# Context attention in bf16 stacks, self-attention splits read from PSUM, and two streams merged by a table of run lengths

## The chip, the cores and the metric

The kernel runs on one core of one Trainium2 chip. The metric is the device time of one launch in microseconds (us). The kernel before took 3042.41 us, the median of three runs between 3033.93 and 3052.46 us.

## What is computed

The reference is a decoder of four layers over x (4 batches, 512 tokens, width 128) with a context of 77 tokens per batch. Each layer has a self attention, a cross attention and a feed-forward part, twelve stages in all, and after each stage the sum with x is normalised. The stages that the change touches are these (cut):

```python
# self attentions of layers 0 and 1: 16 heads of width 8, causal; layer 3 adds biases and a rotation of q and k
scores = softmax(q @ k.T * HD ** -0.5 (causal));  out = scores @ v
# cross attentions of layers 1 and 2: 16 heads of width 8, 512 queries against the 77 context tokens
qh = x @ wq + bq;  kh = ctx @ wk + bk;  vh = ctx @ wv + bv
out = softmax(qh @ kh.T * scale) @ vh;  x = layernorm(x + out @ wo + bo)
```

## The kernel before

**Streams.** Batches 0 and 2 form stream 0, batches 1 and 3 form stream 1; each stream runs its two batches one after the other through the twelve stages of `STAGES` (L2444) and `add_norm` (L373) after each. Each stream owns four PSUM banks and its own buffers, so the streams share only the engines. Every stage is a `Program`: for each engine a generator that issues instructions between `yield`s of due times, numbers that its author planned by hand.

**Order.** `weave` (L293) merges the two streams on each engine: it issues the part whose due time is lowest, with stream 1's times put back by `LAG` = 60 (L26, L2554 to L2570). Each engine then runs its instructions in that one order, and a wait at its head holds up both streams.

**Self attention** (`attention8`, L463; stages l0_attn, l1_attn, l3_attn). q and k are projected as f32 (L524), copied from PSUM by ScalarE (L620, or L622 with a bias), and split into three bf16 parts each: keys by GpSimd, queries by VectorE (`split_up`, L657 to L668); ScalarE repeats parts (L637). SyncE lays six parts and two pad slots out as stacks of 128 rows for each pair of heads (24 transfers, L606 and L608), so that one bf16 matmul gives an exact score. Scores (L552) have their maxima taken by VectorE (L718 causal, L721 otherwise); the negated maxima are split, turned (L557) and written as rows into the query stacks (L613). A second pass computes the scores transposed (L569), ScalarE takes the exponentials (L648), GpSimd masks (L691), TensorE multiplies with the values (L579).

**Context attention** (`attention8_context`, L1308; stages l1_xattn and l2_xattn, so eight times in a launch). ScalarE makes four copies of q with the other heads zeroed (L1419), VectorE the masked keys (L1449). A score unit is one f32 matmul of 308 columns (L1374, 16 of them), whose maxima VectorE takes (L1461). The maxima are split once (L1464 to L1469), turned (L1379) and copied (L1424). In the second pass each head has one f32 matmul of 512 columns (L1387) and one bf16 matmul that adds its maximum (L1390); ScalarE takes the exponential (L1431) and TensorE multiplies with the values (L1398). SyncE and GpSimd have no part in it.

**Elsewhere.** `add_norm` has GpSimd compute the inverse deviation (L401, L403) and TensorE turn x (L409). l2_ffn (L2098) has GpSimd sum scores (L2205), VectorE and ScalarE mark them (L2278, L2238) and TensorE add them up (L2179).

Of the kernel before, what the change touches and what calls it, by code (L numbers as in the profile page):

```python
# [10 lines left out]
BF16 = mybir.dt.bfloat16  # L11
# [5 lines left out]
P = 128  # L17
B, T, D = 4, 512, 128
TJ = T // P
LC = 77  # L20
# [5 lines left out]
LAG = 60.0  # L26
# [5 lines left out]
PAIR_GROUPS = ((0, 1), (1, 2), (2, 4), (4, 8))  # L32
HEADS8, HD8 = 16, 8


def host_constants():
# [14 lines left out]
    c["quadcol"] = np.kron(np.eye(4, dtype=np.float32), np.ones((32, 1), np.float32))  # L51
    c["quadhalf"] = 0.5 * c["quadcol"]
    selhead = np.zeros((P, 4, 4, LC), np.float32)
    for q in range(4):
        for g in range(4):
            selhead[32 * q + 3 * g:32 * q + 3 * g + 3, q, g, :] = 1
    c["selhead"] = selhead.astype(mybir.dt.np(BF16))
# [235 lines left out]
def weave(tracks):  # L293

    heads = []
    for i, steps in enumerate(tracks):
        t = next(steps, None)
        if t is not None:
            heads.append((t, i, steps))
    while heads:  # L300
        head = min(heads, key=lambda h: h[0:2])
        heads.remove(head)
        t, i, steps = head
        after = next(steps, None)
        if after is not None:
            assert after >= t - 1e-6, (t, after)
            heads.append((after, i, steps))
# [155 lines left out]
def attention8(s, wq, wk, wv, scale, causal=False, bq=None, bk=None, bv=None, rope=False, wo=None, first_wait=None):  # L463

    H, G, KC = HEADS8, HEADS8 // 4, TJ
    T1 = 16.0 if rope else 10.0
# [6 lines left out]
        qk_projected=2, v_projected=1 if wv is not None else 0, qk_biased=2, rotated=2 if rope else 0, rope_chain=4 if rope else 0,  # L473
# [125 lines left out]
    def sync(sp):  # L599
        yield T1 - 2  # L600
# [14 lines left out]
    def scalar(a):  # L615
        for q, bias in ((1, bk), (0, bq)):
            yield 2 - q
            a.wait_ge(*qk_projected(2 - q))
            if bias is None:
                a.copy(qk[:, q, :], bank[q][:]).then_inc(qk_biased.sem, 1)  # L620
            else:
                a.activation(qk[:, q, :], bank[q][:], ACT.Identity, bias=bias).then_inc(qk_biased.sem, 1)  # L622
        yield 3
# [8 lines left out]
        for n in range(2):  # L632
            for q, name, split, repeated in ((1, "k", keys_split, keys_repeated), (0, "q", queries_split, queries_repeated)):
                yield T1 - 5 + 2 * n + 0.5 * (1 - q)
# [21 lines left out]

    def split_up(eng, q, done):  # L657
# [12 lines left out]
    def gpsimd(g_):  # L670
# [5 lines left out]
        yield T1 - 6  # L676
        g_.wait_ge(*(roped if rope else qk_biased)(1))
        for _ in split_up(g_, 1, keys_split):
            yield T1 - 4
# [14 lines left out]
    def vector(v):  # L694
# [8 lines left out]
        yield T1 - 4  # L703
        v.wait_ge(*(roped if rope else qk_biased)(2))
        for _ in split_up(v, 0, queries_split):
            yield T1 - 3
# [601 lines left out]
def attention8_context(s, wq, wk, wv, scale, bq, bk, bv, wo, bo, query_mask=None):  # L1308

    H, G, nk = HEADS8, HEADS8 // 4, LC  # L1310
    x_ready, xT_ready, mask_ready = s.x_ready, s.xT_ready, s.mask_ready
    units = [(j, q) for j in range(TJ) for q in (0, 2, 1, 3)]
    D1, D2 = 0.6, 1.7
    T1 = 6.0
    plan = []
    for n in range(len(units)):
        plan += [(T1 + D1 * n, "score", n), (T1 + D1 * n + 1.0, "max", n)]
    Tm = T1 + D1 * len(units) + 1.0
    plan += [(Tm, "split", 0), (Tm + 1.5, "turn", 0), (Tm + 2.2, "rows", 0)]
    T2 = Tm + 3.0  # L1320
    for m in range(H // 2):
        b = T2 + D2 * m
        plan += [(b, "st", m), (b + 0.8, "exp", m)]
        if m % 2 == 1:
            plan += [(b + 2.2, "pv", m // 2), (b + 3.0, "gather", m // 2), (b + 3.6, "out", m // 2), (b + 4.2, "att", m // 2)]
    plan.sort(key=lambda step: step[0])
    end = plan[-1][0]
    (projected, q_ready, keys_ready, v_ready, scores_ready, scores_read, chain, max_split, max_turned, max_copied, st_ready, exp_done, pv_done,
# [18 lines left out]
    def score_bank(u):  # L1347
        return bank[u % 4][:, 0:4 * nk]
# [4 lines left out]
    def group(n):  # L1353

        return n // 2 % 2 + 2 * (n % 2)
# [1369 lines left out]
```

## Time and profile before

| quantity | value |
|---|---|
| median of three runs | 3042.41 us |
| the profiled execution, its own time | 3028.01 us |
| span of its instructions | 3026.3 us |
| TensorE busy | 2467.5 us |
| VectorE busy | 1779.2 us |
| ScalarE busy | 1301.2 us |
| GpSimd busy | 688.8 us |
| granted TensorE clock, mean share of full speed | 0.891 |

The span runs from the first to the last instruction of the profiled execution, its own time has 1.7 us more around it, and the median of the runs lies 14.4 us above that. Busy time is the union of an engine's instructions. PE is TensorE, PEld its weight loads, DVE is VectorE, ACT ScalarE, POOL GpSimd, SP SyncE. An f32 matmul leaves two records.

### The profile page before, as it was taken

Reading aid. Unit: us, or ns where it says so; the run is one execution under the profiler, and the core shown is the slowest. Engines: PE = TensorE matmul, PEld = TensorE weight load, DVE = VectorE, ACT = ScalarE, POOL = GpSimd, SP = SyncE. Lnnn points to the kernel's source line nnn. Section 1 sums busy time; section 2 is a strip of 40 time slices with the busy share of each in tenths; the row PEclk is TensorE's granted clock in tenths of the full one; section 3 lists DMA queues with packets and bytes.
Section 4 is the critical chain, followed back from the end, with each engine's and each line's share of the span. In section 5 each row is a group of like instructions: output and inputs, shape, how many; then the busy total and the mean of one; then the engine's idle time right before and its main releaser. Section 6 shows DMA issues by size and latency. Waiting matters only on the chain.

```text
span 3026.3 us, 38307 instructions
## 1 busy us (share of the span) xinstructions
PE 2467.5 (82%) x12965; PEld 1261.6 (42%) x12965; DVE 1779.2 (59%) x4880; ACT 1301.2 (43%) x3060; POOL 688.8 (23%) x922
## 2 busy tenths in 40 slices
PE   4798998789987887887659888987999888778875
PEld 2333335433443585234323333353344447743242
DVE  5645436664575598744566544486357547987164
ACT  1556622344324542574424556214423344435741
POOL 2430002221112584100123200013201137830000
PEclk7899999779987999999879998988799889999987
DMA  5200001210000002200121000022001000021000
GB/s 167 48 1 1 1 1 33 59 20 16 25 30 1 1 1 57 57 1 32 30 55 20 1 1 1 1 54 56 1 22 35 14 1 1 29 57 29 1 1 7
DMA packets 43595, 73.33 MB, mean 24 GB/s; under 512 B 4420, under 2 KB 36228, under 8 KB 41608
## 3 DMA queue, kind: packets, MB, share of 16 engines
q1 hardware_dynamic: 42824, 69.60, 9.5%
q8 instruction: 103, 1.69, 0.2%
q10 hardware_dynamic: 576, 1.29, 0.1%
q14 instruction: 92, 0.75, 0.1%
HBM read 43.86 MB, written 1.05 MB: 15 GB/s over the span
## 4 chain that ended last, share of the span: by engine, by line
PE 59%; DVE 19%; ACT 10%; issue 7%; POOL 2%; DMA 1%; SPq 1%; ACTq 0%; DVEq 0%; POOLq 0%
PE psum L579 4%; PE psum L1009 4%; PE psum L2179 4%; PE psum L569 3%; PE psum L1020 3%; DVE floor_s L2278 3%; ACT PT_s L1041 2%; PE psum L1557 2%; PE psum L1374 2%; PE psum L1387 2%; DVE mx_s L721 2%; PE psum L552 2%; PE psum L833 2%; PE psum L1848 2%; PE psum L759 2%
## 5 line engine op out<-in xcount | busy, mean ns | idle before, releaser
L648 ACT ACTIVATE PT_s<-psum 128x512 f32<-128x512 f32 (+3 forms) x768 | 343.8, 500 | 242.1 <-PE psum L569 240.0
L401 POOL TENSOR_SCALAR ve<-mv 128x4 f32<-128x4 f32 x48 | 13.4, 280 | 1525.5 <-DVE mv L391 1525.3
L552 PE MATMUL psum<-KS_s,QS_s 128*128 128x512 bf16 (+3 forms) x768 | 236.1, 368 | 104.2 <-DMA KS_s<-parts_s 42.3
L2205 POOL TENSOR_TENSOR buffer<-sim_s 128x1024 f32<-128x1024 f32 x128 | 269.7, 2122 | 152.9 <-DVE floor_s L2278 87.2
L718 DVE CUSTOM_DVE_ANT_0 rest_s<-psum,packed_early 128x128 f32<-128x128 f32 (+3 forms) x512 | 224.4, 488 | 57.9 <-PE psum L552 56.3
L569 PE MATMUL psum<-QS_s,KS_s 128*128 128x512 bf16 (+3 forms) x768 | 233.2, 353 | 28.9 <-ACT PT_s L648 14.8
L579 PE MATMUL psum<-PT_s,vaug 128*9 128x512 f32 (+3 forms) x1536 | 173.5, 526 | 67.4 <-POOL PT_s L691 53.5
L691 POOL TENSOR_SCALAR_AFFINE_SELECT PT_s<-PT_s 128x128 f32<-128x128 f32 x512 | 147.5, 299 | 351.1 <-ACT PT_s L648 346.3
L2238 ACT ACTIVATE above_s<-buffer,below_s 128x1024 f32<-128x1024 f32 x128 | 145.8, 1152 | 125.8 <-PE psum L2179 90.8
L1059 ACT ACTIVATE PT_s<-psum 128x512 f32<-128x512 f32 (+1 forms) x224 | 121.2, 593 | 163.2 <-PE psum L1011 163.1
L721 DVE TENSOR_REDUCE mx_s<-psum 128x1 f32<-128x512 f32 x256 | 159.9, 687 | 37.8 <-PE psum L552 37.8
L2179 PE MATMUL psum<-packed_early,above_s 128*128 128x128 f32 x1024 | 141.9, 284 | 47.9 <-DVE floor_s L2278 40.6
L552 PEld LDWEIGHTS psum<-KS_s,QS_s 128*128 128x128 bf16 x768 | 78.3, 105 | 231.1 <-DVE mx_s L718 79.8
L2278 DVE TENSOR_SCALAR floor_s<-buffer,thr_s 128x1024 f32<-128x1024 f32 x128 | 158.3, 1268 | 10.6 <-POOL buffer L2205 8.6
L569 PEld LDWEIGHTS psum<-QS_s,KS_s 128*128 128x128 bf16 x768 | 69.9, 101 | 222.1 <-ACT PT_s L648 127.1
L2179 PEld LDWEIGHTS psum<-packed_early,above_s 128*128 128x128 f32 x1024 | 121.0, 146 | 68.3 <-issue 53.3
L2179 PE MATMUL psum<-packed_early,floor_s 128*128 128x128 f32 x1024 | 139.1, 281 | 0.0
L415 ACT COPY xT<-psum 128x512 f32<-128x512 f32 x44 | 25.8, 587 | 258.2 <-PE psum L409 258.2
L1041 ACT ACTIVATE PT_s<-psum,low_s 128x77 f32<-128x77 f32 x384 | 121.2, 387 | 5.0 <-DVE low_s L1079 4.4
L2179 PEld LDWEIGHTS psum<-packed_early,floor_s 128*128 128x128 f32 x1024 | 122.1, 146 | 0.0
L1077 DVE TENSOR_REDUCE low_s<-psum 128x1 f32<-128x512 f32 x128 | 82.5, 684 | 49.3 <-PE psum L987 48.8
L1036 ACT ACTIVATE PT_s<-psum,low_s 128x512 f32<-128x512 f32 x128 | 87.9, 692 | 46.3 <-DVE low_s L1077 46.1
(441 smaller groups left out, 4932.4 us busy)
## 6 DMA issues: line engine op xcount, KB each, us to landing
buffer<-packed_experts SPq DMA_DIRECT2D x36, 384.0 KB, 3.3
QS_s<-parts_s SPq DMA_DIRECT2D x96, 128.0 KB
KS_s<-parts_s SPq DMA_DIRECT2D x192, 64.0 KB
buffer<-packed_moe SPq DMA_DIRECT2D x4, 2048.0 KB, 8.5
buffer<-packed_cross SPq DMA_DIRECT2D x4, 2048.0 KB, 7.6
buffer<-packed_product SPq DMA_DIRECT2D x4, 1024.0 KB, 4.8
packed_early<-packed_early SPq DMA_DIRECT2D x1, 2654.0 KB, 12.5
raw_s<-packed_setup SPq DMA_DIRECT2D x1, 1840.0 KB, 7.1
```

Of the source, the lines that this page charges most:

```text
L552: pe.matmul(bank[n % 4][:, 0:n_keys], QS[:, h // 2, j * P:(j + 1) * P], KS[:, h % 2, h // 2, 0:n_keys], start=True, stop=True).then_inc(ri ...
L569: pe.matmul(bank[u % 3][:, q0_of(c):T], KS[:, h % 2, h // 2, c * P:(c + 1) * P], QS[:, h // 2, q0_of(c):T], start=True, stop=True).then_in ...
L579: mm = pe.matmul(OUT[32 * i:32 * i + 9, q0_of(c):T], vaug[:, c, 4 * g + i, :], PT[:, u % 2, i, q0_of(c):T], start=(c == 0), stop=(c == KC ...
L648: a.activation(PT[:, u // 4 % 2, i, q0_of(c):T], bank[u % 3][:, q0_of(c):T], ACT.Exp, scale=scale).then_inc(exp_done.sem, 1)
L691: g_.affine_select(out=blk, in_=blk, compare_op=ALU.is_ge, fill=0.0, base=0, pattern=[[1, P]], channel_multiplier=-1).then_inc(exp_masked. ...
L718: v.tensor_tensor_reduce(junk[:, u % 2, 0:w], bank[n % 4][:, 0:w], s.w["causal"][:, T - w:T], 1.0, -3e38, ALU.add, ALU.max, mx[:, j, h:h + ...
L721: v.tensor_reduce(mx[:, j, h:h + 1], bank[n % 4][:], AX_X, ALU.max).then_inc(scores_read.sem, 1)
L1041: ins = a.activation(junk[:, n * LC:(n + 1) * LC], tail_scores(u)[:, jj, o], ACT.Exp, bias=low[:, 0, row, col:col + 1], scale=-1.0, accum_ ...
L2179: mm = pe.matmul(CT[:, c * P:(c + 1) * P], rows[:, n % KEPT, c * P:(c + 1) * P], s.w["ident"][:], is_transpose=True, start=(h == 0 and i = ...
L2205: g.tensor_tensor(fs[:, n % 2], m[:, 0, :].unsqueeze(2).to_broadcast([P, NK, NK]), m[:, 1, :].unsqueeze(1).to_broadcast([P, NK, NK]), ALU. ...
L2238: a.activation(above[:, n % KEPT, :], total, ACT.Relu, bias=below[:, j % 2, h:h + 1]).then_inc(risen.sem, 1)
L2278: v.tensor_scalar(floor[:, n % KEPT, :], total, thr[:, j % 2, h:h + 1], thr[:, j % 2, h:h + 1], ALU.is_ge, ALU.mult).then_inc(marked.sem, 1)
```

## The change

Three things change. **The order:** `weave` no longer looks at due times; it takes a string of run lengths for each engine (`TURNS`, 1568 numbers for TensorE, 632 for ScalarE, 762 for VectorE, 104 for GpSimd, 48 for SyncE), and issues so many parts of stream 0, so many of stream 1, and so on. `LAG` goes. **Self attentions without rotation** (l0_attn, l1_attn): ScalarE's two copies go; VectorE makes the first part and the rest of both q and k straight from PSUM (`split_projected`), then the other parts of q; GpSimd makes the last two parts of k (`split_rest`). **Context attention** gets the stacks of the self attention: q and k are split into three bf16 parts each, SyncE lays them out (8 transfers for the keys, 8 for the queries), a score unit is two bf16 matmuls of 154 columns with 128 rows, the maxima are split, turned and written as rows in two halves (2 transfers), and the second pass has one bf16 matmul of 512 columns for each head. The constants `quadcol` and `selhead` go, `paritycol` comes. The core of the diff:

```diff
-LAG = 60.0
+TURNS = {
+    "tensor": (
+        "3 3 82 3 2 4 21 4 2 2 4 2 2 2 6 2 2 2 8 2 2 4 6 2 3 2 8 6 4 6 10 6 3 2 10 8 3 2 10 4 3 3 8 4 18 6 3 4 10 4 3 9 10 4 3 4 8 4 8 6 10 "
...
+    "gpsimd": (
+        "2 2 321 140 13 8 13 4 5 30 5 84 1 13 1 80 72 2 82 1 34 1 13 1 8 1 149 148 5 21 1 13 1 177 1 1 9 6 2 1 2 2 25 1 2 1 3 8 1 2 1 2 1 1 "
+        "1 23 2 2 4 1 343 1 9 2 7 359 3 2 69 4 281 140 5 51 5 20 2 148 1 1 9 6 2 1 2 2 28 1 2 9 1 2 1 4 1 2 1 20 2 2 1 1 1 1 "
+    ),
+    "sync": (
+        "2 2 1 1 149 149 358 358 256 209 42 31 1 16 3 45 49 50 129 42 64 151 297 207 63 153 209 208 86 1 63 149 256 209 44 31 1 16 1 45 49 "
+        "50 129 42 64 151 208 208 "
+    ),
+}
...
-def weave(tracks):
...
+def weave(tracks, turns):
+
+    for steps in tracks:
+        next(steps)
+    for n, turn in enumerate(turns.split()):
+        for _ in range(int(turn)):
+            next(tracks[n % STREAMS], None)
+    assert all(next(steps, None) is None for steps in tracks)
...
 def attention8(s, wq, wk, wv, scale, causal=False, bq=None, bk=None, bv=None, rope=False, wo=None, first_wait=None):
...
+    def split_projected(v, q, done):
+        first = parts[:, FIRST_SLOT["qk"[q]][0], q, :]
+        v.wait_ge(*qk_projected(2 - q))
+        v.tensor_copy(first, bank[q][:]).then_inc(done.sem, 1)
+        v.wait_ge(*done(1))
+        v.tensor_tensor(rest[:, q, :], bank[q][:], first, ALU.subtract).then_inc(done.sem, 1)
+
+    def split_rest(eng, q, done):
+        second, third = (parts[:, n, q, :] for n in FIRST_SLOT["qk"[q]][1:])
+        eng.wait_ge(*done(2))
+        eng.tensor_copy(second, rest[:, q, :]).then_inc(done.sem, 1)
+        eng.wait_ge(*done(3))
+        eng.tensor_tensor(third, rest[:, q, :], second, ALU.subtract).then_inc(done.sem, 1)
...
 def attention8_context(s, wq, wk, wv, scale, bq, bk, bv, wo, bo, query_mask=None):
...
-                pe.matmul(score_bank(u), qG[half(q // 2), q, j * P:(j + 1) * P], keys[half(q // 2)].rearrange("p h n -> p (h n)"),
-                          start=True, stop=True, tile_position=(64 * (q // 2), 0)).then_inc(scores_ready.sem, 1)
+                for i in range(2):
+                    mm = pe.matmul(score_bank(u)[:, 2 * i * nk:2 * (i + 1) * nk], QS[:, 2 * q + i, j * P:(j + 1) * P],
+                                   KS[:, 2 * q + i].rearrange("p o n -> p (o n)"), start=True, stop=True)
+                mm.then_inc(scores_ready.sem, 1)
...
-                for o in range(2):
-                    pe.matmul(bank[o][0:nk, :], keys[half(o), u // 2, :], qG[half(o), u % 2 + 2 * o, :], start=True, stop=False,
-                              tile_position=(64 * o, 0))
-                for o in range(2):
-                    pe.matmul(bank[o][0:nk, :], s.w["selhead"][half(o), u % 2 + 2 * o, u // 2, :], nmT[half(o), :], start=False, stop=True,
-                              tile_position=(64 * o, 0)).then_inc(st_ready.sem, 1)
...
+                pe.matmul(bank[u % 2][0:nk, :], KS[:, u // 2, u % 2, :], QS[:, u // 2, :], start=True, stop=True).then_inc(st_ready.sem, 1)
...
+    def sync(sp):
+        yield T1 - 5
+        sp.wait_ge(*keys_pads(1))
+        sp.wait_ge(*keys_split(4))
+        sp.wait_ge(*keys_repeated(2))
+        for i in range(PAIRS):
+            sp.dma_start(KS[:, i], key_parts[2 * HD8 * i:2 * HD8 * (i + 1)]).then_inc(keys_loaded.sem, 16)
+        yield T1 - 2
+        sp.wait_ge(*queries_pads(1))
+        sp.wait_ge(*queries_split(4))
+        sp.wait_ge(*queries_repeated(2))
+        for loaded, (first, last) in zip(pairs_loaded, CONTEXT_GROUPS):
+            for i in range(first, last):
+                sp.dma_start(QS[:, i, :], parts[2 * HD8 * i:2 * HD8 * (i + 1)]).then_inc(loaded.sem, 16)
+        for t, kind, u in plan:
+            yield t
+            if kind == "spread":
+                sp.wait_ge(*max_copied(u + 1))
+                sp.dma_start(QS[FILLED::MAX_STEP, 4 * u:4 * u + 4, :], nmT[:, u, :]).then_inc((first_rows, last_rows)[u].sem, 16)
+
+    def gpsimd(g):
...
+        for n in range(FILLED, SLOTS):
+            ins = g.tensor_copy(key_parts[:, n], own)
+        ins.then_inc(keys_pads.sem, 1)
+        g.memset(parts[:, FILLED:SLOTS, :], 0.0).then_inc(queries_pads.sem, 1)
+        g.memset(nm[:], 0.0).then_inc(rows_pads.sem, 1)
...
     def scalar(a):
-        yield 2
-        a.wait_ge(*projected(2))
-        a.wait_ge(*q_ready(1))
-        for q in range(4):
-            a.activation(qG[:, q, :], bank[0][:], ACT.Identity, bias=bqG[:, q:q + 1], scale=s.w["quadcol"][:, q:q + 1]).then_inc(q_ready.sem, 1)
+        for n in range(2):
+            yield T1 - 6 + 1.5 * n
+            a.wait_ge(*queries_split(2 * n + 1))
+            to = parts[:, MORE_SLOTS["q"][n], :]
+            a.copy(to, parts[:, FIRST_SLOT["q"][n]:FIRST_SLOT["q"][n] + 1, :].to_broadcast(to.shape)).then_inc(queries_repeated.sem, 1)
...
-                    weave([track(s.programs, lambda p: p.tensor, pe, LAG * s.index) for s in streams])
+                    weave([track(s.programs, lambda p: p.tensor, pe, 0.0) for s in streams], TURNS["tensor"])
```

## Rows read from the trace of the kernel before

**Rows 1.** The page: span, busy time of each engine, slices, chain by engine.
```profile
span 3026.3 us, 38307 instructions
...
PE 2467.5 (82%) x12965; PEld 1261.6 (42%) x12965; DVE 1779.2 (59%) x4880; ACT 1301.2 (43%) x3060; POOL 688.8 (23%) x922
...
PEclk7899999779987999999879998988799889999987
...
PE 59%; DVE 19%; ACT 10%; issue 7%; POOL 2%; DMA 1%; SPq 1%; ACTq 0%; DVEq 0%; POOLq 0%
```

**Rows 2.** Stretches: length, busy PE, PEld, DVE, ACT, POOL, granted clock, DMA share, GB/s.
```profile
0.00:80.00 80.00, 37.09 (x128) 19.70 (x128) 48.05 (x162) 10.42 (x28) 22.52 (x19) 0.78 0.57 174
...
640.00:820.00 180.00, 166.31 (x791) 73.47 (x791) 82.30 (x259) 69.48 (x148) 23.28 (x72) 0.87 0.04 12
...
960.00:1220.00 260.00, 212.50 (x1451) 162.26 (x1450) 200.13 (x431) 110.63 (x132) 149.76 (x80) 0.95 0.08 17
...
1360.00:1600.00 240.00, 165.43 (x815) 83.25 (x815) 130.62 (x415) 92.83 (x289) 38.92 (x72) 0.83 0.18 41
1600.00:1860.00 260.00, 233.38 (x1302) 95.85 (x1301) 134.31 (x359) 149.48 (x427) 39.78 (x108) 0.96 0.01 3
...
2860.00:3026.00 166.00, 108.46 (x504) 63.09 (x500) 83.63 (x208) 53.05 (x196) 7.51 (x11) 0.80 0.01 4
```

**Rows 3.** Groups on TensorE, shapes apart: busy us, mean ns, idle before.
```profile
L1374 PE MATMUL psum<-keys_s,qG_s 64*128 64x308 f32 x256 | 84.1, 572 | 12.3 <-DVE mx_s L1461 9.3 <-DVE vaug L1453 3.0
...
L1387 PE MATMUL psum<-qG_s,keys_s 64*77 64x512 f32 x256 | 75.0, 664 | 17.2 <-ACT PT_s L1431 15.8 <-ACT nmT_s L1424 1.4
...
L569 PE MATMUL psum<-QS_s,KS_s 128*128 128x512 bf16 x384 | 141.9, 411 | 21.6 <-DVE mx_s L718 12.5 <-ACT PT_s L648 8.2
...
L569 PE MATMUL psum<-QS_s,KS_s 128*128 128x256 bf16 x128 | 33.7, 287 | 3.2 <-ACT PT_s L648 2.5
...
L1390 PE MATMUL psum<-nmT_s,c_selhead 64*77 64x512 bf16 x128 | 26.0, 400 | 0.0
...
L569 PE MATMUL psum<-QS_s,KS_s 128*128 128x128 bf16 x128 | 25.3, 231 | 4.1 <-ACT PT_s L648 4.1
...
L557 PE MATMUL psum<-packed_early,nm_s 128*32 128x128 f32 x96 | 16.7, 303 | 2.9 <-DVE mx_s L721 1.9 <-DVE nm_s L731 1.0
...
L1379 PE MATMUL psum<-packed_early,nm_s 128*128 128x128 f32 x32 | 7.0, 357 | 4.1 <-DVE nm_s L1467 4.1
```

**Rows 4.** Groups on ScalarE and VectorE, shapes apart.
```profile
L1461 DVE TENSOR_REDUCE mx_s<-psum 128x4 f32<-128x308 f32 x128 | 56.4, 474 | 72.2 <-PE psum L1374 71.7
...
L1419 ACT ACTIVATE qG_s<-psum,bqG_s,packed_early 128x512 f32<-128x512 f32 x32 | 22.3, 779 | 10.8 <-PE psum L1361 7.5 <-DVE bqG_s L1446 3.4
...
L620 ACT COPY qk_s<-psum 128x512 f32<-128x512 f32 x16 | 9.4, 588 | 10.4 <-PE psum L524 10.4
```

**Rows 5.** The tile parts_s: durations min/median/max in ns, first and last start.
```profile
L608 SPq DMA_DIRECT2D KS_s<-parts_s x192: 604/636/2215, 42.7 to 2746.1; - x192
L606 SPq DMA_DIRECT2D QS_s<-parts_s x96: 567/1284/1642, 42.0 to 2744.1; - x96
...
L663 POOL TENSOR_TENSOR rest_s<-qk_s,parts_s x12: 1152/1157/1594, 37.2 to 2713.8; 128x512 f32<-128x512 f32 x12
L661 DVE CAST parts_s<-qk_s x12: 395/623/1993, 38.1 to 2716.0; 128x512 bf16<-128x512 f32 x12
...
L663 DVE TENSOR_TENSOR rest_s<-qk_s,parts_s x12: 693/698/2274, 38.7 to 2716.8; 128x512 f32<-128x512 f32 x12
```

**Rows 6.** Who waited for whom: us in total, times, longest us.
```profile
POOL ve L401 <- DVE mv L391: 1525.3, 44, 106.5
```

**Rows 7.** One context stage of stream 1 beside stream 0's l1_ffn, columns as Rows 2.
```profile
737.00:805.00 68.00, 65.37 (x309) 31.05 (x307) 37.62 (x95) 22.49 (x41) 0.00 (x0) 1.00 0.07 23
```

More of the change, by code:

```diff
@@ L615, in scalar @@
     def scalar(a):
[L616 to L621, printed above, removed]
+        if rope:
+            for q, bias in ((1, bk), (0, bq)):
+                yield 2 - q
+                a.wait_ge(*qk_projected(2 - q))
                 a.activation(qk[:, q, :], bank[q][:], ACT.Identity, bias=bias).then_inc(qk_biased.sem, 1)
-        yield 3
+        yield 3 if rope else 2
         if wv is not None:
@@ L675, in gpsimd @@
         g_.memset(nm[:], 0.0).then_inc(pads_set.sem, 1)
[L676 to L679, printed above, removed]
+        if rope:
+            yield T1 - 6
+            g_.wait_ge(*roped(1))
+            for _ in split_up(g_, 1, keys_split):
+                yield T1 - 4
+        else:
+            yield 3
+            split_rest(g_, 1, keys_split)
         g_.wait_ge(*keys_split(4))
@@ L1319, in attention8_context @@
[L1319 to L1325, printed above, removed]
+        if n % (U // 2) == U // 2 - 1:
+            at, u = T1 + D1 * n + 1.0, n // (U // 2)
+            plan += [(at, "split", u), (at + 1.9, "turn", u), (at + 2.6, "rows", u), (at + 3.2, "spread", u)]
@@ L1326, in attention8_context @@
+    T2 = T1 + D1 * U + 1.0
+    for n in range(H):
+        plan += [(T2 + D2 * n, "st", n), (T2 + D2 * n + 0.7, "exp", n)]
+    for u in range(G):
+        at = T2 + D2 * (4 * u + 3) + 1.5
+        plan += [(at, "pv", u), (at + 0.8, "gather", u), (at + 1.4, "out", u), (at + 2.0, "att", u)]
     plan.sort(key=lambda step: step[0])
     end = plan[-1][0]
[L1328 to L1332 removed]
@@ new lines, in gpsimd @@
+    def gpsimd(g):
+        own = s.w["paritycol"][:].unsqueeze(2).to_broadcast([P, 2, nk])
+        yield 0
+        g.wait_ge(*xT_ready)
+        for n in range(FILLED, SLOTS):
[3 more added lines that the diff above has]
+        g.memset(nm[:], 0.0).then_inc(rows_pads.sem, 1)
+        yield 2
+        first, second, third = (key_parts[:, n] for n in FIRST_SLOT["k"])
+        g.wait_ge(*keys_apart(1))
+        g.tensor_copy(first, keys[:]).then_inc(keys_split.sem, 1)
+        g.wait_ge(*keys_split(1))
+        g.tensor_tensor(keys_left[:], keys[:], first, ALU.subtract).then_inc(keys_split.sem, 1)
+        to = key_parts[:, MORE_SLOTS["k"][0]]
+        g.tensor_copy(to, first.unsqueeze(1).to_broadcast(to.shape)).then_inc(keys_repeated.sem, 1)
+        g.wait_ge(*keys_split(2))
+        g.tensor_copy(second, keys_left[:]).then_inc(keys_split.sem, 1)
+        g.wait_ge(*keys_split(3))
+        g.tensor_tensor(third, keys_left[:], second, ALU.subtract).then_inc(keys_split.sem, 1)
+        g.tensor_copy(key_parts[:, MORE_SLOTS["k"][1]], second.unsqueeze(1)).then_inc(keys_repeated.sem, 1)
```

183 lines of the change are left out of this document (101 added, 82 removed), and 51 rows, old and new, of the table TURNS.

## The prediction

> **What bounds the kernel now.** I read the page first, then the span cut into stretches at the stages' ends, then the groups on TensorE with shapes kept apart, then tiles and waits. The page [rows 1] shows TensorE busy for 2467.5 us of 3026.3, VectorE for 59% and ScalarE for 43%, and a chain that lies 59% on TensorE, 19% on VectorE and 10% on ScalarE. So TensorE is the bound, but it is idle for 3026.3 - 2467.5 = 559 us, and only two things can make the kernel faster: less work on TensorE, or less idle time. The stretches [rows 2] show where the idle time lies. The first 80 us are setup and the lone start of stream 0: 43 us idle. The seam between the two batches (1360 to 1600 us) has 75 us, and the end (2860 to 3026 us), where stream 1 finishes alone, 58 us. The remaining 559 - 43 - 75 - 58 = 383 us are spread over 2540 us, 15.1%; the best stretch, 640 to 820 us, has 13.7 of 180, 7.6%. A third quantity is the granted clock: 0.96 in the dense stretch 1600 to 1860 us, 0.83 in the seam, so part of the 2467.5 us is work at the lower of two levels.
>
> **Context attention, TensorE.** It goes through eight stages. What goes is L1374, L1387 and L1390 [rows 3]: 84.1 + 75.0 + 26.0 = 185.1 us. What comes are 128 score units of two bf16 matmuls with 154 columns, 128 bf16 matmuls with 512 columns, and twice the turns. No row has a 154-column bf16 matmul. A unit has 308 columns in all, so the nearest row is L569 with 256 columns: 33.7 / 128 = 0.26 us, which I stretch to 0.29 us, or 37 us for 128. From below: 308/512 of L1390's 26.0 / 128 = 0.20 us, or 0.12 us, 16 us in all; from above: two of L569's 128-column matmuls, 25.3 / 128 = 0.20 us each, 51 us. The second pass has 512 columns: at most L569's 141.9 / 384 = 0.37 us, 47 us, at least L1390's 26 us; I take 37 us, the middle, because matmuls of this pass alternate with waits in some stages and not in others. The turns: 64 of L557's kind (16.7 / 96 = 0.17 us) for 32 of L1379's (7.0 us), +4 us. New work is 78 us (46 to 102 us), so **TensorE loses 107 us of work** (83 to 139 us).
>
> Whether that is worth its face value depends on what lies beside it. The context stage of stream 1 runs beside stream 0's l1_ffn, and there TensorE is busy for 65.4 of 68 us [rows 7]: every microsecond saved is taken up by l1_ffn. I count the 107 us in full.
>
> **Context attention, the other engines.** ScalarE loses the four masked copies (L1419, 22.3 us [rows 4]) and gains two copies per stage. VectorE still takes 128 maxima of 308 columns (L1461, 56.4 us), which is now the pace of the score pass, 16 x 0.474 = 7.6 us against some 16 x 0.66 = 10.5 us of TensorE before. It gains four operations on 128x512 per stage, of 0.62 to 0.70 us [rows 5], 8 x 2.6 = 21 us in all, and three more small splits; GpSimd gains two pads, two memsets and six small operations. None of these engines is the bound, so I put these edits at nothing; their cover is the other stream's work on TensorE, and if that is gone they cost their duration, at most some 5 us a stage.
>
> The new latency is ahead of the first score. SyncE issues eight key transfers at 0.64 us and the first two query transfers at 1.28 us [rows 5], 7.7 us, behind a split of about 3 us on VectorE and a copy. From below it costs nothing, when the other stream keeps TensorE busy; from above 8 x 10 = 80 us. In the score and second passes the stage gets shorter by as much (3 us, and half of the second pass's matmul time), so I take nothing. TensorE's new wait for all keys stands ahead of the stage's scores; behind it in the queue are the other stream's next parts, as the table puts them. GpSimd's wait for the masked keys has the other stream's masks (L691) behind it, and TensorE's value products wait for those.
>
> VectorE's cast of a part takes 395 to 1993 ns and its subtraction 693 to 2274 ns at the same shape [rows 5], while GpSimd has work at the same time in these stages. By the Trainium skill ("SBUF — State Buffer", Who interferes with whom) GpSimd and VectorE share a pair of ports that one instruction holds to its end, and a VectorE instruction with two SBUF inputs contends with a GpSimd one that reads SBUF, which speaks against new GpSimd work beside the query split. By that rule the four query operations could each take the maximum; I read the spread as such a wait: (1.37 + 1.58) x 2 x 8 = 47 us more on VectorE, which would stretch the latency ahead of the first score and add at most that to the sum. I leave it out because VectorE is not the bound, and because the subtractions of the self attentions now read PSUM with one SBUF operand.
>
> **Self attentions.** L620 goes from ScalarE, 9.4 us [rows 4] in eight stages, with GpSimd's cast and its subtraction of 1.16 us [rows 5]; VectorE gains a cast and a subtraction, about 1.3 us a stage. The stacks are ready perhaps 1.5 us sooner, since the key split no longer waits for ScalarE and half of it leaves the slower engine. Eight times 1.5 us is 12 us, but it is latency that the other stream mostly covers: I count it at nothing (0 to 12 us).
>
> **The order.** Here is the larger term and the less certain one. I counted the steps of every stage and laid the run lengths over them. On TensorE both streams start together now (before, stream 1 began when stream 0 had issued 152 of the 358 parts of its first attention). At the seam, stream 1 begins its last stage when stream 0 is 167 parts into the next attention, instead of 19. Stream 1's l2_ffn begins when stream 0 has issued 39 of its 44 parts, instead of 23, so the two stages heavy on VectorE and GpSimd (960 to 1220 us: 200 and 150 us of 260 [rows 2]) no longer overlap. At the end both streams are in their last stage together: stream 1 starts it at stream 0's fifth part of ten. TensorE changes stream 1567 times instead of 2815. No row prices an order, so I bound it by the best and the worst stretch: from nothing, to all stretches but the first at 7.6%, which would be 0.076 x 2946 + 43 = 267 us of idle time and a gain of 292 us. I take each place by itself. The seam goes to the average of 15.1%, 36 of 240 us: 39 us gained. The end loses a third of its 58 us: 20 us. The 383 us go half the way to the best stretch, to 11.35%: 288 us, 95 us gained. Together **154 us of idle time**.
>
> **Clock.** The mean is 0.891, the dense stretch has 0.96 [rows 2]. If TensorE idles less it may stay at the higher level longer; a fifth of the way, 0.905, would take 2360 x (1 - 0.891/0.905) = 37 us off. Matmuls that stand alone carry a latency that does not go with columns, so I take 20 us; the bounds are 0 and 150 us, the whole way.
>
> **Sum.** Against the profiled execution's 3028 us (span 3026.3 and 1.7 around it): 3028 - 107 - 154 - 20 = 2747 us. The median of the runs lies 14 us above that execution, within their spread, so I take 2750 us as the measured time.
>
> **Rivals.** *The records do better than I grant*: all stretches near the best one, so 3028 - 107 - 250 - 40 = 2631 us. For it speaks that TensorE is 90% busy wherever both streams have work; against it, that the order is fixed beforehand and real durations vary, as VectorE's do [rows 5]. Chance 0.22. *The order is worth nothing*: the table only swaps one fixed order for another, the idle time stays, and the context stages' new latency takes back a third: 3028 - 70 = 2958 us, or somewhat under 2900 us where the order gives a little. For it speaks that the fixed lag already reaches 90% in places; against it the seam and the end. Chance 0.18. *Slower, by one blocked queue*: the table puts long runs of one stream ahead on GpSimd (343 parts of stream 0's attention ahead of stream 1's normalisation at the seam, then 359 of stream 1). `add_norm` needs GpSimd for the inverse deviation, and GpSimd already stands at it for 1525 us, up to 106.5 us at a time [rows 6]. If that wait stands ahead of the other stream's masks, or behind them, both streams stop. With the order's other gains kept it decides when a normalisation costs TensorE over (107 + 154) / 44 = 6 us on average, without them from 107 / 44 = 2.4 us on; at 4 us for each of 44 and no gain from the order the time is 3028 - 107 + 176 = 3097 us. Chance 0.07. *The change does not do what it says*: the runs were made from records of another kernel, and the gains cancel with stalls, about 3030 us. Chance 0.03.
>
> **How the numbers follow.** The forecast itself (2660 to 2860 us) has 0.50. Its own range comes from the context term (83 to 139 us) and half to one and a half of the order term. The range of 2600 to 2900 us takes in the better rival down to 2600 us and the part of the order's failure under 2900 us; about 0.06 lies below and 0.13 above. Half a percent, 15 us, is about what a measurement of this kernel can tell from no change. Faster: 0.50 + 0.22 + 0.18 = 0.90, less 0.02 for the order's failure with new stalls, 0.88; same 0.03; slower 0.09.
>
> **What would show it.** Right, if the page of the changed kernel shows TensorE's busy time at 2320 to 2380 us, the context stages' matmuls at about 78 us, idle time near 400 us, the seam at 15% idle or less, and a clock of 0.90 or more. The context term is wrong if these matmuls take over 110 us, or if TensorE waits for the stacks' transfers over 5 us a stage. The order term is wrong if idle time is over 520 us or under 300 us. The blocked queue would show as long waits of GpSimd's L691 or of the inverse deviation followed by waits of TensorE in both streams.

## The result, and the profile after

The changed kernel takes **2790.4 us** (median of four runs, 2789.0 to 2793.4) against 3038.2 us before (median of four: the three runs known beforehand and one more): a ratio of 0.918, 95% interval 0.914 to 0.921. The forecast was 2750 us in a range of 2600 to 2900 us.

The page of the changed kernel's profiled execution (2789.0 us, span 2787.3), lines as in [rows 1]:

```profile
span 2787.3 us, 38246 instructions
...
PE 2331.1 (84%) x12741; PEld 1222.4 (44%) x12741; DVE 1817.1 (65%) x4984; ACT 1273.3 (46%) x3036; POOL 699.8 (25%) x986
...
PEclk7899999799997999999789999987989799999986
...
PE 26%; DVE 12%; ACT 6%; issue 4%; SPq 2%; POOL 2%; DMA 1%; POOLq 0%; DVEq 0%; ACTq 0%
```

TensorE is busy for 2331.1 us instead of 2467.5, 136 us less, and idle for 2787.3 - 2331.1 = 456 us instead of 559, 103 us less. The clock is 0.914 instead of 0.891. TensorE's share of the chain fell from 59% to 26%, but the shares of this chain add up to only 53% of the span, so I read the amounts of work and idle time instead.

The context stages' groups on TensorE, shapes apart (columns as in [rows 3]):

```profile
L1480 PE MATMUL psum<-QS_s,KS_s 128*77 128x512 bf16 x128 | 48.1, 426 | 5.2 <-DVE mx_s L1599 2.8 <-ACT PT_s L1562 1.9
...
L1462 PE MATMUL psum<-KS_s,QS_s 128*128 128x154 bf16 x256 | 30.6, 238 | 17.5 <-DMA QS_s<-parts_s 8.6 <-DVE mx_s L1599 8.3
...
L1470 PE MATMUL psum<-packed_early,nm_s 128*32 128x128 f32 x64 | 10.6, 292 | 4.7 <-DVE nm_s L1609 4.7
```

They take 30.6 + 48.1 + 10.6 = 89 us where the groups that they replace took 84.1 + 75.0 + 26.0 + 7.0 = 192 us [rows 3]: 103 us less.

The stretches of the start, the seam and the end (columns as in [rows 2]):

```profile
0.00:80.00 80.00, 37.20 (x126) 20.33 (x126) 45.82 (x142) 13.81 (x35) 27.96 (x24) 0.77 0.62 179
...
1300.00:1500.00 200.00, 165.08 (x868) 85.84 (x867) 134.68 (x411) 85.20 (x281) 47.95 (x92) 0.84 0.22 51
...
2700.00:2787.00 87.00, 51.36 (x233) 32.30 (x229) 60.10 (x145) 14.89 (x36) 5.18 (x7) 0.73 0.02 7
```

The start has 43 us of idle time, as before. The seam has 35 us in 200 (17%) instead of 75 in 240 [rows 2], the last 87 us have 36, where the last 166 had 58. The rest, 2420 us, has 456 - 43 - 35 - 36 = 342 us, 14.1%, where 2540 us had 383, 15.1%. These stretches are shorter than those of before. At the same lengths, 240 us around the seam (1300 to 1540) have 41 us of idle time (17%) and the last 166 us have 46: 34 and 12 us less than before.

GpSimd's wait for the means, in the view of who waited for whom, got shorter [rows 6]:

```profile
POOL ve L457 <- DVE mv L447: 1234.2, 41, 84.7
```

### The profile page after: what moved, and what is told of

It reads as the page before. It is cut to its first block, busy times and chain, and to the rows that moved or that the text cites. A ratio compares the mean times of both kernels' runs of the same rounds, so it can differ in the third digit from the quotient of the medians.

```text
span 2787.3 us, 38246 instructions
## 1 busy us (share of the span) xinstructions
PE 2331.1 (84%) x12741; PEld 1222.4 (44%) x12741; DVE 1817.1 (65%) x4984; ACT 1273.3 (46%) x3036; POOL 699.8 (25%) x986
## 4 chain that ended last, share of the span: by engine, by line
PE 26%; DVE 12%; ACT 6%; issue 4%; SPq 2%; POOL 2%; DMA 1%; POOLq 0%; DVEq 0%; ACTq 0%
ACT PT_s L1121 2%; PE psum L1089 2%; PE psum L635 2%; DVE mx_s L801 2%; PE psum L2321 2%; PE psum L625 1%; PE psum L1699 1%; DVE floor_s L2420 1%; PE psum L1100 1%; PE psum L913 1%; PE psum L839 1%; PE psum L1990 1%; PE psum L1067 1%; PE psum L608 1%; PE psum L1976 1%
## 5 line engine op out<-in xcount | busy, mean ns | idle before, releaser
L702 ACT ACTIVATE PT_s<-psum 128x512 f32<-128x512 f32 (+3 forms) x768 | 331.1, 501 | 204.1 <-PE psum L625 201.7
L2347 POOL TENSOR_TENSOR buffer<-sim_s 128x1024 f32<-128x1024 f32 x128 | 258.3, 2029 | 145.1 <-DVE floor_s L2420 100.7
L608 PE MATMUL psum<-KS_s,QS_s 128*128 128x512 bf16 (+3 forms) x768 | 214.9, 364 | 68.0 <-DVE mx_s L798 26.8
L625 PE MATMUL psum<-QS_s,KS_s 128*128 128x512 bf16 (+3 forms) x768 | 204.1, 345 | 34.2 <-ACT PT_s L702 19.4
L2420 DVE TENSOR_SCALAR floor_s<-buffer,thr_s 128x1024 f32<-128x1024 f32 x128 | 149.0, 1183 | 31.2 <-PE psum L2321 25.4
L608 PEld LDWEIGHTS psum<-KS_s,QS_s 128*128 128x128 bf16 x768 | 72.6, 102 | 203.0 <-DVE mx_s L798 84.4
L1121 ACT ACTIVATION_READ_ACCUMULATOR PT_s<-psum,low_s 128x1 f32 x384 | 105.0, 335 | 0.0
L2012 ACT ACTIVATE act_s<-psum 128x512 f32<-128x512 f32 x72 | 43.0, 597 | 129.9 <-PE psum L1986 128.6
## 6 DMA issues: line engine op xcount, KB each, us to landing
packed_early<-packed_early SPq DMA_DIRECT2D x1, 2653.0 KB, 12.5
```

What stands on the lines that cost most here:

```text
L608: pe.matmul(bank[n % 4][:, 0:n_keys], QS[:, h // 2, j * P:(j + 1) * P], KS[:, h % 2, h // 2, 0:n_keys], start=True, stop=True).then_inc(ri ...
L625: pe.matmul(bank[u % 3][:, q0_of(c):T], KS[:, h % 2, h // 2, c * P:(c + 1) * P], QS[:, h // 2, q0_of(c):T], start=True, stop=True).then_in ...
L702: a.activation(PT[:, u // 4 % 2, i, q0_of(c):T], bank[u % 3][:, q0_of(c):T], ACT.Exp, scale=scale).then_inc(exp_done.sem, 1)
L1121: ins = a.activation(junk[:, n * LC:(n + 1) * LC], tail_scores(u)[:, jj, o], ACT.Exp, bias=low[:, 0, row, col:col + 1], scale=-1.0, accum_ ...
L2347: g.tensor_tensor(fs[:, n % 2], m[:, 0, :].unsqueeze(2).to_broadcast([P, NK, NK]), m[:, 1, :].unsqueeze(1).to_broadcast([P, NK, NK]), ALU. ...
L2420: v.tensor_scalar(floor[:, n % KEPT, :], total, thr[:, j % 2, h:h + 1], thr[:, j % 2, h:h + 1], ALU.is_ge, ALU.mult).then_inc(marked.sem, 1)
```

## The experiments

"Stages" says whose attention stages the kernel has, "order" how the streams are merged; busy, idle and clock are TensorE's in the profiled execution, idle being the span less the busy time.

| run | stages | order | us (median) | ratio to before | busy | idle | clock |
|---|---|---|---|---|---|---|---|
| before | before | lag 60 | 3033 to 3043 | 1 | 2467.5 | 558.8 | 0.891 |
| ctx_lag | context changed | lag 60 | 3002.8 | 0.986 to 0.993 | 2367.9* | 627.5* | 0.883 |
| self_lag | self changed | lag 60 | 3019.8 | 0.991 to 0.996 | 2470.1* | 548.0* | 0.886 |
| both_lag | changed | lag 60 | 2987.4 | 0.982 to 0.987 | 2383.8* | 610.0* | 0.884 |
| lag_0 | changed | lag 0 | 3344.9 | 1.100 to 1.106 | 2429.7 | 913.4 | 0.825 |
| after | changed | its table | 2790.4 | 0.914 to 0.921 | 2331.1 | 456.2 | 0.914 |
| oldself_table | context changed | its table | 2796.8 | 0.919 to 0.923 | 2320.6* | 472.7* | 0.914 |
| before_own_table | before | table of mine | 2791.0 | 0.917 to 0.922 | 2387.1 | 398.1 | 0.930 |
| after_own_table | changed | table of mine | 2730.3 | 0.898 to 0.902 | 2301.4 | 425.7 | 0.932 |
| own_table_again | changed | second table | 2752.0 | 0.905 to 0.910 | 2320.0 | 424.9 | 0.927 |
| lag_split | transfers cut | lag 60 | 3030.9 | 0.997 to 0.999 | 2393.2 | 638.3 | 0.879 |
| after_split | transfers cut | its table | 2842.5 | 0.934 to 0.938 | 2350.3 | 496.1 | 0.905 |
| split_own_table | transfers cut | table of mine | 2770.4 | 0.911 to 0.916 | 2338.7 | 436.7 | 0.922 |
| after_halves | transfers reordered | its table | 2778.3 | 0.912 to 0.917 | 2308.6* | 463.7* | 0.919 |

In the rows with a star 81 to 85 matmul records of the self attentions are missing from the trace. In lag_split, which has all, these groups take 472.1 us; in both_lag 449.1. So there up to 23 us stand as idle instead of busy. The kernel before was run again beside each group of runs, which is why its median is a range; differences under some 10 us between rows of different groups lie within that range.

### The parts one by one, under the order of before

ctx_lag is the kernel before with the context attention's hunks alone, self_lag with those of the self attentions, both_lag with both; the due-time order stays. The hunks bring their own due times (a context stage's first score is due at 10 instead of 6, a self attention's at 8 instead of 10), so the merge around them shifts a little as well.

```diff
 LAG = 60.0
+CONTEXT_GROUPS = ((0, 2), (2, 4), (4, 6), (6, 8))
...
-def attention8_context(s, wq, wk, wv, scale, bq, bk, bv, wo, bo, query_mask=None):
...
+def attention8_context(s, wq, wk, wv, scale, bq, bk, bv, wo, bo, query_mask=None):
...
```

> The kernel before with the context attention's change alone; self attentions and the due-time order (lag 60) as before. My theory: the work saved on TensorE is worth its face value under any order, so 3038 - 103 = 2935 us (2905 to 2960), TensorE busy about 2365 us, idle time as before within 30 us. Rival A (the latency ahead of the first score is paid under an order that was not made for these stages): TensorE's busy time falls as much, but its idle time rises by 40 to 80 us, so 2975 to 3015 us.

> The kernel before with the self attentions' change alone (projection split by VectorE from PSUM, ScalarE's copy left out). My theory: 0 to 12 us faster, 3026 to 3038 us; TensorE's busy time unchanged, ScalarE's smaller by about 9 us, the spread of VectorE's cast and subtraction (395 to 1993 and 693 to 2274 ns) gone in the self attentions, still there in the context ones. Rival B (the shorter way to the stacks is a good part of the saved idle time): 40 us or more faster, under 3000 us.

> The changed kernel's stages under the order of the kernel before (due times, stream 1 behind by 60). My theory: the order is what took some 100 us of idle time away, and some of the clock's gain with it, so 2920 us (2890 to 2950), idle time 530 to 580 us, TensorE busy 2340 to 2370 us. Rival C (the order is worth little, the saved idle time comes from the new stages themselves): 2790 to 2840 us. Rival A again: above 2970 us.

My theory fell for the context stages, and rival A held: 3036.2 - 3002.8 = 33 us, not 103. TensorE's groups, then its wait for the queries' stack, in ctx_lag:

```profile
L1396 PE MATMUL psum<-QS_s,KS_s 128*77 128x512 bf16 x128 | 51.1, 427 | 15.5 <-DVE mx_s L1515 9.8 <-ACT PT_s L1478 5.2
...
L1378 PE MATMUL psum<-KS_s,QS_s 128*128 128x154 bf16 x256 | 42.0, 282 | 49.8 <-DMA QS_s<-parts_s 37.5 <-DVE mx_s L1515 11.2
...
L1386 PE MATMUL psum<-packed_early,nm_s 128*32 128x128 f32 x64 | 11.4, 308 | 0.7 <-DVE nm_s L1525 0.7
```

```profile
PE psum L1378 <- DMA QS_s<-parts_s: 37.5, 13, 5.6
```

The work did go: 42.0 + 51.1 + 11.4 = 105 us for 192. But idle time rose by 46 to 69 us (627.5 - 558.8, less what the missing records may hold), and 37.5 us of it stand at one wait that the kernel before does not have: the scores', for the stack of the queries. Each of the eight stages has it, with 2.4 to 5.6 us at its first score, also the stage of stream 1 beside stream 0's l1_ffn, which I had taken from [rows 7] as the model of a covered one. That stage's timeline in ctx_lag, TensorE first, then VectorE (start us, length us; in brackets the idle time before and who ended it):

```profile
730.65 1.95 PE L1892 MATMUL psum<-buffer,hT_s 128*128 128x128 f32 x16
736.50 0.30 PE L1378 MATMUL psum<-KS_s,QS_s 128*128 128x154 bf16 x2 [3.90 <-DMA QS_s<-parts_s]
736.64 1.16 PE L1902 MATMUL psum<-xT,buffer 128*128 128x512 f32 x2
```

```profile
730.99 0.69 DVE L1961 TENSOR_TENSOR hT_s<-sg_s,psum 128x512 f32<-128x512 f32 x1
...
736.84 0.48 DVE L1515 TENSOR_REDUCE mx_s<-psum 128x4 f32<-128x308 f32 x1 [3.07 <-PE psum L1378]
```

The next matmul of l1_ffn (L1902) had its inputs: VectorE's last result for it (L1961) was done at 731.7, and its weights were issued at 727.0 at the latest, where such transfers take at most 4.3 us to land in this stretch. It starts at 736.64, right behind the first score. So the cover that I had named, the other stream's work on TensorE, was there, but it stood behind the waiting score in TensorE's queue.

VectorE plays a smaller part. In the first context stage it takes stream 0's four query operations (L1498 to L1504) ahead of maxima of stream 1, for which TensorE waits 4.42 us:

```profile
645.48 0.75 DVE L1498 TENSOR_SCALAR parts_s<-psum,packed_late 128x512 bf16<-128x512 f32 x1
```

```profile
650.24 1.44 PE L565 MATMUL psum<-QS_s,KS_s 128*128 128x512 bf16 x3 [4.42 <-DVE mx_s L714]
```

The four operations take 2.6 us of these. Over the whole run the waits of this kind rose from 12.5 us [rows 3] to 17.9, so they account for some 5 of the 46 to 69 us.

The self attentions' part gave 16 us, a little over my 0 to 12; TensorE's wait for their stacks fell from 42.3 to 28.0 us, which is most of it. Under the table it is 6.4 us (below). Both together gave 3036.2 - 2987.4 = 49 us, which is 33 + 16; 2987.4 us lie above my 2890 to 2950 and fit rival A once more. So of the 248 us **the order is worth 2987.4 - 2790.4 = 197 us**. The two profiled executions lie 207 us apart: 131 to 154 us of idle time, and 53 to 76 us by which the same matmuls got shorter.

> The changed kernel with the self attentions of before, its table of runs changed only so far that each of their steps stands where its counterpart stood. My theory: the split is worth 0 to 12 us here too, 2790 to 2805 us. Rival B: over 2830 us.

It took 2796.8 us, as expected. The intervals of its ratio and of the changed kernel's overlap (0.919 to 0.923 and 0.914 to 0.921), so the 6.4 us are not clear of nothing.

What the order took away shows in TensorE's waits in both_lag and then in the changed kernel (us in total, times, longest):

```profile
PE psum L405 <- DVE x L391: 52.2, 30, 4.8
PE psum L575 <- POOL PT_s L703: 47.6, 67, 4.2
...
PE psum L1402 <- DMA QS_s<-parts_s: 38.7, 13, 6.0
...
PE psum L1019 <- DVE nm_s L1114: 28.6, 6, 6.8
```

```profile
PE psum L635 <- POOL PT_s L763: 21.7, 37, 2.3
...
PE psum L465 <- DVE x L451: 16.7, 11, 4.0
...
PE psum L1079 <- DVE nm_s L1174: 12.6, 5, 3.5
...
PE psum L1462 <- DMA QS_s<-parts_s: 8.6, 6, 4.8
```

For the normalised x of a stage, for GpSimd's masks, for the queries' stack and for the maxima of the 64-wide attentions TensorE waited 167.1 us under the lag and 59.6 us under the table. No single wait carries the gain: all of TensorE's waits together fell from some 590 to some 437 us, and what the four leave of that lies mostly in waits for maxima and exponentials. These are the places where one stream stands still; that the table has the other's work there is how I read it, and no run takes the places one by one.

### Is it the interleaving, or only the start together?

```diff
-LAG = 60.0
+LAG = 0.0
```

> The changed kernel's stages in due-time order, with both streams starting together (lag 0 in place of 60). My theory: the gain of the table is in the interleaving made from records, not in starting the streams together; with equal due times both streams are in the same stage and ask for the same engines at the same time, so it is slower than with lag 60: over 3050 us. Rival J (the lag itself costs the idle time at the start, the seam and the end, and the table's gain is that it has none): 2850 to 2950 us.

With equal due times it took 3344.9 us, 357 us more than with lag 60. With both streams in the same stage nothing stands beside a stack on its way or a normalisation; TensorE's longest waits in lag_0:

```profile
PE psum L548 <- DMA KS_s<-parts_s: 222.7, 12, 22.6
PE psum L405 <- DVE x L391: 84.7, 50, 5.3
PE psum L1402 <- DMA QS_s<-parts_s: 83.6, 12, 15.0
```

Lags other than 60 and 0 were not tried, so how much of the table's gain a better lag would give stays open.

### The order alone, and a table from the changed kernel's own records

In before_own_table only the order is replaced (the `weave` of the change, with run lengths of mine); in after_own_table only the run lengths differ from the change. The tables were made from the records of the kernel in question: each step's waits, signals and durations were laid out in time, an engine taking the stream whose next step has its inputs, and of two the one with more left to do, plus an offset for each of 24 parts of the run. The offsets were varied some thousand times, and the order that ended first was taken.

```diff
-LAG = 60.0
+TURNS = {
+    "tensor": "3 3 40 1 48 4 14 2 2 2 2 1 28 24 17 3 2 8
...
-def weave(tracks):
+def weave(tracks, turns):
...
```

> The kernel before with all its stages unchanged, and only the order replaced: run lengths that I made from the records of the kernel before (each engine takes the stream whose next step has its inputs; where both have, the one with more left to do, with an offset that varies along the run). My theory: the order pays without the new stages, 2790 to 2860 us, idle time 350 to 430 us, clock above 0.905. Rival G (it pays mainly because it hides the new stages' latency): 2930 to 3000 us. Rival C (an order is worth little): 3020 to 3040 us.

> The changed kernel with run lengths that I made in the same way from its own records. My theory: its table was made from records of other stages and leaves something: 2700 to 2760 us, idle time 370 to 430 us. Rival H (durations vary from run to run as much as a better table could give): 2780 to 2800 us.

Span, busy time and clock of before_own_table:

```profile
span 2785.2 us, 38295 instructions
...
PE 2387.1 (86%) x12965; PEld 1225.4 (44%) x12965; DVE 1791.3 (64%) x4880; ACT 1292.5 (46%) x3060; POOL 683.9 (25%) x922
...
PEclk7899999899999999989889999998999899999986
```

and of after_own_table:

```profile
span 2727.1 us, 38237 instructions
...
PE 2301.4 (84%) x12741; PEld 1210.0 (44%) x12741; DVE 1838.4 (67%) x4984; ACT 1270.7 (47%) x3036; POOL 696.9 (26%) x986
...
PEclk8799999999987999999898999988999799999996
```

Both came as my theory had it. The kernel before, with every stage as it was, takes 2791.0 us under a table of its own, as much as the changed kernel: 247 us from the order alone, 161 us of them idle time and 80 us shorter matmuls (both traces have all records). The changed kernel takes **2730.3 us** with a table from its own records and beats both. Under such tables the new stages are worth 2791.0 - 2730.3 = 61 us: 86 us less work on TensorE, 28 us more idle time. With the second table below in place of the first it is 39 us.

> The changed kernel with run lengths made once more, from the records of after_own_table. My theory: the second round still gains a little, 2705 to 2730 us. Rival H (what is left is the scatter of the durations): 2727 to 2745 us.

It took 2752.0 us, 22 us more than the first table, against my theory and somewhat outside the rival's bounds too. Two tables that were made in the same way for the same stages differ by that much on the chip, so less than some 20 us between tables tells nothing of the stages.

### The latency ahead of the first score: more of it, and less

In lag_split and after_split each transfer of a context stage's stacks is cut in two. A half takes as long to issue as a whole one, 0.60 us (median).

```diff
-            sp.dma_start(KS[:, i], key_parts[2 * HD8 * i:2 * HD8 * (i + 1)]).then_inc(keys_loaded.sem, 16)
+            for o in range(2):
+                sp.dma_start(KS[:, i, o], key_parts[2 * HD8 * i:2 * HD8 * (i + 1), :, o, :]).then_inc(keys_loaded.sem, 16)
...
```

> The changed kernel's stages under the order of before, with each of a context stage's sixteen stack transfers cut in two: SyncE issues ten more transfers of 0.6 us ahead of the first score, about 6 us of added latency in each of eight stages and no added work for TensorE. My theory: the 69 us of idle time that the context stages brought under this order is the latency of the stacks, so nearly all of the added latency is paid too: 2987 + 30 to 50 = 3017 to 3037 us. Rival E (it comes from elsewhere in the new stages, the scores' pace or the second pass): 2985 to 2998 us.

> The changed kernel with the same transfers cut in two, table unchanged. My theory: the new order has work of the other stream beside the stacks, so less than half of the added 48 us is paid: 2795 to 2812 us. Rival F (the latency is paid under the table as well, and was only outweighed): 2825 to 2845 us.

lag_split: 3030.9 - 2987.4 = 43 us of some 48, as my theory had it; TensorE's wait for the queries' stack grew from 38.7 us to this:

```profile
PE psum L1402 <- DMA QS_s<-parts_s: 86.2, 19, 11.5
```

after_split: 2842.5 - 2790.4 = 52 us, where I expected less than 24; here my theory fell and rival F held. TensorE's wait for the queries' stack grew by less than half of that, from 8.6 to 31.2 us. But the wait for all keys stands by itself in TensorE's queue, ahead of the other stream's next parts, and the profile puts it down to the line that comes next there. In the changed kernel these waits are 1.6 + 1.5 = 3.1 us, in after_split 20.3:

```profile
PE psum L1462 <- DMA QS_s<-parts_s: 31.2, 16, 10.5
...
PE psum L1992 <- DMA KS_s<-keyparts_s: 10.7, 2, 5.5
...
PE psum L635 <- DMA KS_s<-keyparts_s: 4.9, 1, 4.9
PE psum L625 <- DMA KS_s<-keyparts_s: 4.7, 1, 4.7
```

Together they grew by 22.6 + 17.2 = 39.8 us, and TensorE's idle time by 496.1 - 456.2 = 39.9. So the added idle time stands at the two waits for this stack. Besides, the matmuls take 19 us longer (2350.3 against 2331.1), at a clock of 0.905 instead of 0.914.

> The changed kernel with its stack transfers cut in two, as in after_split (2842.5 us), but with run lengths made from the records of that run. My theory: a fixed order hides the latency that its records contain and pays any that comes later, so most of the cost of the cut goes away: 2735 to 2775 us, that is at most 45 us above after_own_table (2730.3 us). Rival I (the two streams have no work to lay beside this latency, so it is paid under any order): 2730 + 45 to 55 = 2775 to 2790 us and TensorE still waiting some 30 us for the queries' stack.

A table made for the longer way took 2770.4 us, and TensorE waits for this stack no longer than in after_own_table (13.5 us), also with the 2.0 us for the keys:

```profile
PE psum L1401 <- DMA QS_s<-parts_s: 10.0, 10, 2.7
```

That is 40 us above after_own_table and 18 above own_table_again. The number lies inside my theory's bounds by 5 us, the short wait speaks against rival I, but with 22 us between two tables of the same stages this doesn't say how much of the cut's cost an order can hide. It stays open.

after_halves takes latency away: four keys, four queries, then the others.

```diff
-        for i in range(PAIRS):
+        for i in range(PAIRS // 2):
             sp.dma_start(KS[:, i], key_parts[2 * HD8 * i:2 * HD8 * (i + 1)]).then_inc(keys_loaded.sem, 16)
...
+            if first == PAIRS // 2:
+                for i in range(PAIRS // 2, PAIRS):
+                    sp.dma_start(KS[:, i], key_parts[2 * HD8 * i:2 * HD8 * (i + 1)]).then_inc(more_loaded.sem, 16)
...
```

> The changed kernel and its table, with SyncE's transfers of a context stage in another sequence: the first four key transfers, four query transfers, then the other four key transfers and the other query transfers; TensorE waits for the second half of the keys at the second half of the scores. No work is added or left out; four issues of 0.6 us, 2.4 us, go from the way to the first score in each of eight stages. My theory: as added latency was paid in full under this table (52 us for some 48), latency that is taken away is given back, 2790 - 10 to 20 = 2770 to 2780 us. Rival K (a fixed order made for the longer way has the other stream's work in front of the first score, so an earlier stack is worth nothing): 2786 to 2795 us.

2778.3 us, 12 us less than the changed kernel for some 19 us of latency, which is what my theory had. TensorE's two waits for the stack fell from 8.6 + 3.1 to 3.8 us. The 95% intervals of the two ratios touch (0.912 to 0.917, 0.914 to 0.921), so the sign is likely and the size rough. Together with the table of after_own_table it was not tried.

## Why the prediction held, and where it did not

The direction and the range held; the sum missed by 42 us (2747 against 2789 in the profiled executions): 51 us less idle time went than predicted and 4 us less context work, while the matmuls got 13 us shorter than predicted. Of the signs named for "right", busy time, context matmuls and clock came; idle time (456 us, not near 400) and the seam (17%, not 15% or less) did not.

- **Context work on TensorE**: 107 us predicted, 103 measured; that it is so close is partly luck. The scores were put at 37 us and took 30.6. The second pass was put at 37 us, the middle of 26 to 47, and took 48.1, just over the upper bound, which was L569's price for 512 columns [rows 3]. The two errors partly cancel: 78.7 us for 74. The turns cost 3.6 us more, for 4.
- **"From below it costs nothing, when the other stream keeps TensorE busy; from above 8 x 10 = 80 us ... so I take nothing"**: this step failed. Under the old order the new stages brought 46 to 69 us of idle time, near the upper bound. The reason that I gave for zero was a stage of stream 1 beside l1_ffn [rows 7], where TensorE has work for every microsecond. That work does not count as cover when it stands behind the waiting score in an in-order queue: in ctx_lag this very stage waits 3.90 us with l1_ffn's next matmul ready. I also looked for the price as TensorE's wait for the stacks (at most 5 us a stage). In the changed kernel that wait is 8.6 us for the queries and 3.1 for the keys in all, 1.5 us a stage, and would have cleared the term, while after_split shows that 48 us of further latency cost 52.
- **Order**: 154 us of idle time predicted, 103 seen between the two profiles, with whatever the stages' latency costs in the same number. Alone the order took away 131 to 154 us with the new stages (both_lag to the changed kernel) and 161 us with the old ones. By place: the seam 40 us (39 predicted), the end 22 (20), the rest 383 - 342 = 41 us where I had 95; with stretches of the same length as before it is 34, 12 and 57 us. The rest went from 15.1% to 14.1%, not to 11.35%. Whether the order gave less there than I took, or the stages' latency took it back, is not shown: no run has the change's table with the context stages of before.
- **Clock**: 20 us predicted. Busy time fell by 136 us, 103 of them context work, so 33 us went to shorter matmuls; by the order alone it is 53 to 80 us, while under the old order, with the new stages' idle time, the clock was lower, 0.883 in ctx_lag. The step guessed a fifth of the way to the best stretch's clock, 0.905; the changed kernel has 0.914.
- **Self attentions**: 0 to 12 us predicted and counted at nothing; 16 us under the lag, 6 us under the table, which is not clear of nothing.
- **Median**: the 14 us between the profiled execution and the median were left out of the 2750 us; in the changed kernel the two are 1.4 us apart.
- **Query transfers**: I took 1.28 us to issue each, from the self attentions' row [rows 5]; the new ones take 0.61 us. The error was on the safe side and the latency was dear all the same.
- **The port of GpSimd and VectorE**: the two operations of the self attentions that now read PSUM have lost the spread of [rows 5]; of the context ones two read PSUM and take 750 to 751 ns in the changed kernel, so the four could not each take the maximum; the last reaches 847 ns, in ctx_lag 2280 ns. The 47 us that I had left out did not show in the changed kernel:

```profile
L714 DVE CAST parts_s<-psum x16: 680/691/692, 35.8 to 1919.8; 128x512 bf16<-128x512 f32 x16
L716 DVE TENSOR_TENSOR rest_s<-psum,parts_s x16: 691/691/693, 36.5 to 1920.5; 128x512 f32<-128x512 f32 x16
...
L1586 DVE CAST parts_s<-left_s x8: 426/467/479, 628.9 to 2256.1; 128x512 bf16<-128x512 f32 x8
L1588 DVE TENSOR_TENSOR parts_s<-left_s,parts_s x8: 691/693/847, 629.4 to 2256.5; 128x512 bf16<-128x512 f32 x8
```

  The Trainium skill ("SBUF — State Buffer", Who interferes with whom) has VectorE contend with GpSimd for its second SBUF input or in a two-port mode, not with one SBUF input alone; the steady 691 to 693 ns of L716, which reads PSUM and one SBUF tile, agree (the second of them, at 38.14 us, runs beside a subtraction of GpSimd and takes 0.69 us).
- **Rivals**: that the order is worth nothing is refuted by 197 and 247 us. That the records do better than I granted was half true: a better table gave 2730 us, not 2631. GpSimd was not blocked, since its wait fell from 1525 to 1234 us. lag_0 shows what a bad order can cost: 3344.9 - 3033.1 = 312 us over the kernel before.

## What to carry to other kernels

When two streams share in-order queues, price a shorter computation by the work that it saves on the bound engine less the latency that it puts ahead of that engine, and look at what stands behind the wait in the queue: the other stream's work is no cover there, even when it is ready. Add up a profile's waits by what is waited for, over all lines, since one wait can be put down to several. Try the order by itself before the stages: here run lengths made from the records gave the whole gain without any change of the computation, and the changed stages gave 49 us under the old order and 39 to 61 under such tables. A fixed order is made for the latencies in its records, so make it again after each change of a stage, and take differences under a per cent between two such orders for scatter (22 us in the one pair that was tried).

## What the runs showed of the hardware

TensorE's 12741 matmul records of the changed stages take 2301.4 us at a mean granted clock of 0.932 (after_own_table), 2331.1 at 0.914 (after), 2393.2 at 0.879 (lag_split) and 2429.7 at 0.825 (lag_0): in these four, the more idle time (426, 456, 638 and 913 us), the lower the clock and the longer the same matmuls. It is no exact rule: own_table_again, with 425 us of idle time, has 0.927 and 2320.0 us. Span, busy time and clock of lag_0:

```profile
span 3343.1 us, 38229 instructions
...
PE 2429.7 (73%) x12741; PEld 1321.4 (40%) x12741; DVE 1867.9 (56%) x4984; ACT 1245.1 (37%) x3024; POOL 718.2 (21%) x986
...
PEclk8798898687967897698868999975979679967987
```

The issue of a 128 KB transfer of queries takes SyncE 1313 ns in the self attentions and 608 ns in the context ones (median; the bytes are the same, the source's layout is not), in the changed kernel's tile QS_s. The self attentions' key transfers, from the same source layout as their queries but of 64 KB, take 640 ns; no run varies layout and size apart.

```profile
L662 SPq DMA_DIRECT2D QS_s<-parts_s x96: 582/1313/1693, 47.0 to 2532.5; - x96
L1517 SPq DMA_DIRECT2D QS_s<-parts_s x64: 544/608/1154, 636.8 to 2268.7; - x64
```

VectorE's cast of a part from SBUF spreads from 715 to 1995 ns in the rotated self attentions of self_lag, while the same cast from PSUM stays within 678 to 693 ns in all sixteen:

```profile
L658 DVE CAST parts_s<-psum x16: 678/686/693, 35.8 to 2063.4; 128x512 bf16<-128x512 f32 x16
...
L673 DVE CAST parts_s<-qk_s x4: 715/1356/1995, 1156.6 to 2704.8; 128x512 bf16<-128x512 f32 x4
```
